# New hand-written orders for the four engines of a two-layer decoder kernel, with finer waits between its stages

## The reference, cut to what is computed

```python
x = x + L0_attn(layernorm(x))      # delta rule, 4 heads, RMS norm          } stage AB
x = x + L0_xattn(layernorm(x), ctx, ctx)   # causal, 16 heads of 8          }
x = x + L0_ffn(layernorm(x))       # depth 6: local attention, 16 heads of 64, rotary,
                                   # then a gated GELU layer                  stage C
x = x + L1_attn(layernorm(x))      # cosine attention, 16 heads of 8        }
x = x + L1_xattn(layernorm(x), ctx, ctx)   # mLSTM-like, 8 heads of 16      } stage DE
x = x + L1_ffn(layernorm(x))       # 16 experts, top 3, all experts computed}
```

## Time and profile before

| quantity | value |
|---|---|
| median of 3 runs | 4438.04 us (4435.57 to 4442.29) |
| the profiled execution, first to last instruction | 4433.1 us |
| PE busy, mean granted clock | 4137.5 us (93%), 0.969 |
| DVE, ACT, POOL busy | 3566.6, 3444.4, 2650.6 us |
| stage AB, from the start to its last addition | 0 to 546 us |
| stage C | 546 to 3485 us |
| stage DE | 3485 to 4433 us |

### The profile page before, as it was taken

The page is one execution under the profiler, slowest core; times in us unless marked ns, Lnnn a source line. Parts: engine busy times, 40 slices in busy tenths (PEclk is TensorE's granted clock), DMA queues, the critical chain, the costliest instruction groups (busy, mean ns, idle before and its releaser), DMA issues.

```text
span 4433.1 us, 150676 instructions
## 1 busy us (share of the span) xinstructions
PE 4137.5 (93%) x61520; PEld 3049.0 (69%) x61520; DVE 3566.6 (80%) x11101; ACT 3444.4 (78%) x9647; POOL 2650.6 (60%) x2210
## 2 busy tenths in 40 slices
PE   7999989999999999999999999999999689999999
PEld 5777756666666666666666666666666478888888
DVE  4666599999889888899898989898989357766775
ACT  3555478889888888888888988888888357776776
POOL 3444377777777777777777777777777133333331
PEclk8888899999999999999999999999999789999999
DMA  3000000000000000000000000000000100000000
GB/s 101 4 4 4 4 3 4 5 3 4 29 4 4 4 28 4 4 4 13 20 3 4 5 28 4 4 4 8 7 9 9 47 2 4 4 4 4 4 4 6
DMA packets 65258, 46.43 MB, mean 10 GB/s; under 512 B 29220, under 2 KB 63032, under 8 KB 63800
## 3 DMA queue, kind: packets, MB, share of 16 engines
q1 hardware_dynamic: 64568, 36.78, 2.9%
HBM read 28.48 MB, written 2.10 MB: 7 GB/s over the span
## 4 chain that ended last, share of the span: by engine, by line
PE 68%; ACT 13%; DVE 10%; POOL 5%; issue 5%; SPq 0%; DVEq 0%; DMA 0%; ACTq 0%; POOLq 0%
PE ps L557 56%; PE ps L561 12%; ACT BIG L909 7%; DVE BIG L1109 5%; POOL BIG L1549 5%; ACT L909 2%; ACT BIG L901 2%; DVE sm L1120 2%; ACT ps L901 1%; DVE BIG L1117 1%; DVE BIG L1114 1%; POOL sm L1552 0%; DVE sm L1117 0%; DVE BIG L1187 0%; DVE sm L1113 0%
## 5 line engine op out<-in xcount | busy, mean ns | idle before, releaser
L557 PE MATMUL ps<-WB,BIG 128*128 128x128 f32 (+2 forms) x8576 | 1941.9, 363 | 8.4 <-ACT BIG L901 3.4
L901 ACT ACTIVATE BIG<-ps 128x512 f32<-128x512 f32 (+6 forms) x3168 | 1484.0, 530 | 538.8 <-PE ps L561 407.7
L1549 POOL TENSOR_TENSOR BIG<-BIG,sm 128x512 f32<-128x512 f32 (+1 forms) x864 | 1219.0, 1426 | 788.7 <-DVE sm L1319 473.5
L557 PEld LDWEIGHTS ps<-WB,BIG 128*128 128x128 f32 (+1 forms) x8576 | 1142.2, 193 | 217.6 <-issue 175.6
L561 PEld LDWEIGHTS ps<-t_ident,BIG 128*128 128x128 f32 x6016 | 705.8, 144 | 541.4 <-issue 250.2
L561 PE MATMUL ps<-t_ident,BIG 128*128 128x128 f32 x6016 | 916.2, 282 | 162.5 <-ACT BIG L901 53.3
L1549 POOL TENSOR_TENSOR BIG<-BIG 128x512 f32<-128x512 f32 x768 | 967.2, 1280 | 144.1 <-DVE BIG L1109 144.1
L1120 DVE TENSOR_REDUCE sm<-BIG 128x8 f32<-128x512 f32 (+3 forms) x1472 | 882.6, 611 | 174.5 <-ACT BIG L909 172.2
L557 PEld LDWEIGHTS ps<-BIG 64*64 64x64 f32 (+2 forms) x37888 | 626.0, 130 | 364.6 <-issue 93.1
L557 PE MATMUL ps<-BIG 64*64 64x64 f32 (+4 forms) x37888 | 774.7, 225 | 69.7 <-ACT BIG L901 18.7
L909 ACT ACTIVATE BIG<-ps 128x512 f32<-128x512 f32 (+1 forms) x832 | 512.1, 616 | 257.3 <-PE ps L557 252.3
(11 more groups left out here) (120 smaller groups left out, 2985.1 us busy)
## 6 DMA issues: line engine op xcount, KB each, us to landing
WB<-in_Wqkv SPq DMA_DIRECT2D x6, 1536.0 KB, 7.4
XS<-y_sb SPq DMA_DIRECT2D x96, 63.0 KB
y_sb<-in_ctx SPq DMA_DIRECT2D x16, 256.0 KB, 3.1
WB<-in_Wo SPq DMA_DIRECT2D x6, 512.0 KB, 9.1
x_sb<-in_x SPq DMA_DIRECT2D x8, 256.0 KB, 5.0
WB<-in_F_W SPq DMA_DIRECT2D x1, 2048.0 KB, 8.6
WB<-in_F_W SPq DMA_DIRECT2D x8, 256.0 KB, 6.5
out<-x_sb SPq DMA_DIRECT2D x8, 256.0 KB, 2.3
```

The costliest lines, as they stand in the source:

```text
L557: return te.matmul(o, l, r, start=start, stop=stop, skip_group_check=not check)
L901: return se.activation(o, i, ACT.Copy)
L1549: return pe_.tensor_tensor(o, a, b, op)
```

## The change

All three order tables are new for all engines. The phases and their instructions stay the same, with these exceptions:

- C's first layer norm becomes phases of its own (`d1` to `d4` on DVE, `d` on POOL), run only for depth step 0; `first_norm`, `first_pow` and the two `rot` semaphores go.
- The table of rotary factors is made at DVE's first phase of tile 30 of the step before, not at slot start of tile 0.
- The barriers `all_ab` and `all_c` go. In their place a phase waits for the single phase that last used its buffer (`after_one`, `after_two` and the waits in `dve_de`). PE's banks are handed out through all stages in one pass.
- C's semaphores form a ring of 12 in place of 8, since its units now live for up to 9 slots.
- After the last GELU an ACT table set that holds both logarithm and exponential is loaded by hand.
- The expert weights are loaded in two parts, the first while C's last step runs.
- `SLOT` and `BEGIN` give every phase a number by which an engine's list is sorted. They lie so far apart that the stages stay in sequence on every engine.

The diff, cut to its core:

```diff
 AB_ORDER = {
-    "pe": "J1 b12 V3 s4 O3 a22 u5 b22 T1 o3 a32 w3 t5 G1 b32 D1 p14 a42 v4 x3 b42 X0 q3 Z2 y5 a11 W2 p04",
+    "pe": "V3 b12 s4 O3 u5 a22 o3 b22 T1 w3 a32 b32 G1 a42 D1 b42 v4 x3 X0 p14 t5 q3 Z2 a11 W2 y5 p04 J0",
...
 DE_ORDER = {
-    "pe": "om3 p12 oJ6 p02 av3 u2 hA5 oK6 t2 hO6 oL6 w2 hD5 hN6 oA5 gT5 hP6 oB5 b25 oC5 xc2 hG5 X11 hE5 oM6 g2 hF5 "
-          "oD5 J1 oP6 oN6 oO6 X34 oE5 hI5 hJ5 hH5 oF5 g34 cs2 oG5 hC4 hB4 T1 hK5 G2 s1 hM5 oI5 oH5 hL5 ct2",
-    "act": "h25 xc4 hG7 hE7 X13 kG7 kE7 hF7 g14 sq3 kF7 g24 X36 hI7 kI7 hJ7 hH7 kJ7 x36 kH7 T3 hC6 kC6 hB6 hK7 kB6 "
-           "kK7 e13 ex4 hM7 e03 kM7 hL7 ct4 kL7 p13 em4 p03 t3 hA6 hO7 vc1 kA6 kO7 hD6 hN7 gT6 kD6 hP7 kP7 kN7",
+    "pe": "oP7 hF6 xc3 hG6 oC6 oD6 hI6 oE6 g3 X35 oF6 oG6 hH6 g35 cs3 T2 hC5 hB5 hJ6 G3 s2 hK6 oI6 hM6 hA5 oH6 hL6 "
+          "p12 ct3 hD5 p02 hN6 av3 om3 oJ6 hP6 oL6 u2 oK6 X11 hO6 oM6 t2 gT5 oA5 w2 oN6 b25 J1 oO6 hE5 oB5",
+    "act": "g24 kI7 hH7 x36 kH7 hC6 T3 hJ7 hB6 kC6 kJ7 kB6 hK7 e13 ex4 e03 hM7 kM7 hA6 kA6 kK7 p13 hL7 ct4 hD6 kL7 "
+           "kD6 p03 hN7 kN7 em4 hP7 X12 kP7 t3 hO7 gT6 kO7 sq2 hE6 kE6 xc3 hF6 hG6 kF6 h24 vc3 kG6 X35 g13 hI6",
...
 C_ORDER = {
-    "pe": "2tr3 1v13 2a16 1k12 1p15 2o6 1o6 1b03 1a03 1q01 2g03 2g13 2g23 1b13 1a13 2a03 1v03 2a23 1p04 1q11 "
-          "1y5 1w5 1s3 1x0 1k01",
-    "act": "1b04 1q02 1a04 1b14 2g04 2g14 2g24 1f04 1f14 1a14 1q12 1v04 2sh2 1p05 1o06 1o16 1x1 1k02 1s04 1k12 "
-           "2tr3 1s14 1v13 1p15",
-    "dve": "1first0 1n42 1n52 1n62 1n72 1i14 1n82 2a23 1r01 1q11 1s03 1r11 2a15 1s13 1k01 1l01 1u03 1o5 1k11 "
-           "2sh1 2ag1 1i03 1l11 2o5 2ep1 1u13 1n01 1q00 1n11 1n21 2tr1 1n31 2a02 1second1",
-    "pool": "1first1 1n13 1q12 1k02 1q02 1p04 1k12 2sh2 1p14 1n02",
+    "pe": "1b06 1a06 2g26 2a26 1v06 1b16 2a18 2g16 1a16 1y8 1q14 1w8 1k04 1x3 1v15 2tr5 1s6 1p07 2g07 1k14 1o8 1p17 "
+          "2o8 2a07 1q03",
+    "act": "2sh5 1f07 1q05 1b07 1a07 1s18 1v07 1a17 1b17 1f17 2g27 1q15 2g17 1o09 1o19 1x4 1k05 2tr6 1v16 1p08 2g08 "
+           "1k15 1s07 1p18",
+    "dve": "1q04 1n05 1d10 1n15 1d20 1n25 1n35 1d30 1n45 1i07 1n55 1d41 2a18 2tr5 1u17 2a26 1n65 1n75 1i17 1n85 1r04 "
+           "1q14 1r14 1s06 1s16 2sh4 1k04 2ag4 2ep4 1k14 1o8 2o8 1l14 2a07 1l04 1u06",
+    "pool": "1q16 1n17 2sh6 1q06 1k06 1k16 1p08 1d1 1p18 1n06",
 }
...
+SLOT = {"ab": 14.8, "c": 11.6, "de": 25.4}
+BEGIN = {
+    "ab": {"pe": -0.7, "act": -3.5, "dve": -10.8, "pool": -18.7},
+    "c": {"pe": 1069.1, "act": 1060.6, "dve": 1071.2, "pool": 1059.6},
+    "de": {"pe": 4802.5, "act": 4787.2, "dve": 4783.2, "pool": 4816.1},
+}
...
-        CC = ring_units(kinds, "c", 8)
+        CC = ring_units(kinds, "c", 12)
...
-        def all_ab():
-
-            return [u.on("dve", "y") for u in AB[-8:]]
-
-        def all_c():
-            return all_ab() + [u.on("dve", "x") for u in uC2.values() if u.at["l"] == depth - 1]
-
+        def after_one(u):
+
+            return [AB[29 + 2 * u.at["t"]].on("pe", "w")] if AB and u.at["l"] == 0 and u.at["t"] < 2 else []
...
+        def schedule(e):
+
+            due = []
+            for seq, order, stage in ((AB, AB_ORDER, "ab"), (CC, C_ORDER, "c"), (DE, DE_ORDER, "de")):
+                items = [(o[:-1], int(o[-1])) for o in order[e].split()]
+                for n in range(len(seq) + 10):
+                    for j, (ph, lag) in enumerate(items):
+                        u = unit(seq, n - lag)
...
+                            due.append((BEGIN[stage][e] + SLOT[stage] * (n + j / len(items)), u, ph[1:] if stage == "c" else ph))
+            return [d[1:] for d in sorted(due, key=lambda d: d[0])]
...
+                    if u is last2 and ph == LAST_GELU:
+                        o.then_inc(u.name("act", ph, sems), 1)
+                        se.preload_act_table_set("natural_log_exp_and_others")
+                        return
...
-                        for s in all_c() if t == 0 else [DE[t - 8].on("dve", "xP")] if t >= 8 else []:
-                            w.wait_ge(*s)
+                        if t >= 8:
+                            w.wait_ge(*DE[t - 8].on("dve", "xP"))
+                        elif CC and t < 4:
+                            w.wait_ge(*uC1[(depth - 1, NT - 4 + t)].on("pe", "o"))
+                        elif CC and t == 4:
+                            w.wait_ge(*last2.on("dve", "tr"))
```

More of the change, by code:

```diff
@@ L107 @@
 C_ORDER = {
[7 rows of a table removed]
[7 rows of a table added]
 }
-SILENT = ("first", "second")
+NORM = ("d1", "d2", "d3", "d", "d4")
 for _kind in "12":
@@ L160, in __init__ @@
         self.base = dict(base)
-        self.marks = MARKS["C2f" if at.get("last") else kind]
+        self.marks = MARKS[kind + "f" if at.get("last") or at.get("l") == 0 and kind == "C1" else kind]
         self.count = dict.fromkeys(ENG, 0)
@@ L371, in de_bufs @@
             return b
-        def phases(order, seq, e, n):
-            for o in order[e].split():
-                u = unit(seq, n - int(o[-1]))
-                if u:
-                    yield u, o[:-1]
-        for seq, order, emptied, pairs in ((AB, AB_ORDER, AB_EMPTIED, AB_PAIRS), (DE, DE_ORDER, DE_EMPTIED, DE_PAIRS)):
-            full, turn = [()] * 8, 0
-            for u in seq:
-                u.bank, u.after = {}, {}
-            for n in range(len(seq) + 8 if seq else 0):
-                for u, ph in phases(order, seq, "pe", n):
-                    if ph not in emptied:
-                        u.after[ph] = ()
-                        continue
-                    wide = 1 + (ph in pairs)
-                    turn += turn % wide
-                    u.bank[ph], u.after[ph] = turn % 8, full[turn % 8] + (full[turn % 8 + 1] if wide == 2 else ())
-                    for i in range(wide):
-                        full[(turn + i) % 8] = tuple((u, *m.split()) for m in emptied[ph])
-                    turn += wide
@@ L408, in build, with take @@
+        full, turn, primed = [()] * 8, 0, [(), ()]
+        for u in AB + CC + DE:
             if u:
                 u.bank, u.after = {}, {}
[L410 to L426 removed]
+        def take(u, ph, marks, wide, banks):
+            nonlocal turn
+            turn += turn % wide
+            u.bank[ph], u.after[ph] = turn % banks, ()
+            for i in range(wide):
+                u.after[ph] += full[(turn + i) % banks]
+                full[(turn + i) % banks] = tuple((u, *m.split()) for m in marks)
+            turn += wide
@@ new lines, in build @@
+        order = schedule("pe")
+        places = [i for i, (u, ph) in enumerate(order) if u.stage == "c"]
+        for i, (u, ph) in enumerate(order):
+            banks = 6 if places and places[0] <= i <= places[-1] else 8
+            if places and i == places[0]:
+                primed = [full[6], full[7]]
+            u.after[ph] = ()
+            if u.stage == "ab":
+                if ph in AB_EMPTIED:
+                    take(u, ph, AB_EMPTIED[ph], 1 + (ph in AB_PAIRS), banks)
+            elif u.stage == "de":
+                if ph in DE_EMPTIED:
+                    take(u, ph, DE_EMPTIED[ph], 1 + (ph in DE_PAIRS), banks)
+            elif u.kind == "C1" and ph == "s":
+                u.bank.update({"s0": 6, "s1": 7})
+                full[6], full[7] = ((u, "act", "s0"),), ((u, "act", "s1"),)
+            elif u.kind == "C1" and ph == "y":
+                for h in "01":
+                    take(u, "y" + h, ("act o" + h,), 1, 6)
+                u.after["y"] = u.after["y0"] + u.after["y1"]
+            elif u.kind == "C2" or ph != "w":
+                take(u, ph, EMPTIED[u.kind[1] + ph], 1, 6)
@@ L690, in pe_bank @@
             def pe_bank(u, ph):
[L692 to L695 removed]
+                for v, e, m in u.after[ph]:
                     w.wait_ge(*v.on(e, m))
@@ L1562, in _ @@
             w.wait_ge("const", 2)
+            for r in (0, 64):
+                pe_.memset(XS[r:r + 1, :, 64:128], 0.0)
+            pe_.memset(c2_bufs().hT[64:96, 1024:1536], 1.0).then_inc(sems["ones"], 1)
+            w.wait_ge("ones", 1)
             def pool_ab(u, ph):
```

211 lines of the change are left out of this document (103 added, 108 removed), and 18 rows, old and new, of tables (AB_ORDER, DE_ORDER).

## The result

The changed kernel takes 4381.25 us (median of 4, 4376.92 to 4384.2), and the kernel before, run beside it, 4440.16 us (median of 4, 4435.57 to 4443.65). The ratio is 0.9868, 95% interval 0.9855 to 0.9881. The sign and the range were right, the size was not: 59 us came where I had forecast 147. The profiled execution is 4382.4 us long, at a mean granted clock of 0.963. Lines move with the diff: PE's matmuls L557 are now L564 and its transposes L561 are L568; DVE's L1109 and L1117 are L1126 and L1134; ACT's L901 and L909 are L907 and L915.

What follows compares the result with a forecast made beforehand. PE, busy 93% of the span, was taken as the bound, gains coming only from its idle time. 4433.1 - 55 (DE steady) - 20 (DE first slots) - 72 (C) = 4286.1, so median 4291 us, range 4195 to 4400.

Steps and rivals of the forecast that it cites:

- rival (3): C: ACT falls behind and PE waits before `k0` in each of 192 C1 units; 4536 us at 0.9 us each; chance 0.10.
- the mix: PE: alternating small and large matmuls was taken as free, adding nothing to PE's busy time.
- I count nothing for it: C: keeping DVE's all-SBUF work away from POOL was booked at 0, up to 55 us were DVE the bound.
- The wait goes: DE: PE's 1.20 us wait on DVE's `C` before `ct` vanishes, given 1.4 us more cover.
- My lower bound of 25 us: DE, steady part: the least gain, against 55 us forecast, if the `ct` or `hK` wait returns elsewhere.
- residual 0.35 before `p1`: DE: PE still waits 0.35 us a tile before `p1` for POOL's masked `m1`, bounds 0 and 0.6.
- the 0.15 at `cs`: DE: a new wait of 0.15 us a tile, as `cs3` follows `g3` after five phases, about 1.6 us.
- the first slots: DE's start: splitting one tile's chain over two lags shortens the first slots, gaining 20 us, bounds 0 and 35.
- under 20 us from `T` to `T`: DE's first tiles: a sign of the forecast, successive `T` starts under 20 us apart, against 26.5 us in the old list.
- three waits that I had named: AB: new PE waits before `b2`, `b3` and `a4`; without cover such a pair costs 0.2 to 0.5 us.
- The clock of 0.89 stays: AB: PE's granted clock stays at 0.89, the work around `u` being the same.
- From 4230 to 4345: Whole kernel: reach in us of the main forecast, 4291 us, with the bounds of its terms; chance 0.49.

Runs made afterwards that it cites:

- free banks: The changed kernel with each PE phase of DE taking the PSUM bank that comes free first, instead of the next in rotation: 4353.27 us, ratio 0.977.
- the swap: The changed kernel with DVE's `rg` in DE issued behind `C` instead of ahead of it: 4373.82 us, ratio 0.982.
- the profile in which it was short by itself: The changed kernel with eight PE phases of AB put back in the old sequence: 4435.55 us, ratio 0.9966.
- both experiments with small edits: The changed kernel with eight AB phases of PE in old sequence (4435.55 us), and, separately, with PE's `w` moved between `a3` and `b3` (4402.78 us).

## Why the prediction was wrong, point by point

The length of a phase "in its turn" is counted from the end of the phase ahead of it on PE to its own end, so that a wait is part of it.

- **C, the steady group.** Right: 58.8 us (forecast 58.7), no wait of 1.1 us, and rival (3), `k0` waiting for `v0`'s bank, did not occur. It came out right partly by luck, by two terms that I had wrong and that cancel: PE's idle time fell by more than forecast (82 us, not 72), and its busy time in a group rose from 57.8 to 58.2 us by the mix, which I took as free.
- **C, the borders of the steps.** The failed step: "I count nothing for it", of VectorE and GpSimd colliding. The diff moved six small products into POOL's busy stretch, and I put no price on where they went, though the earlier trace rows had the price of one, up to 1149 ns. It costs 22 us of C, nearly all at four of the five borders, shown by moving them away. Without it C would have come out at -71.
- **DE, `ct` and the bank.** The failed step: "The wait goes". It left `ct` (1.86 us in its turn before, 0.44 after), but a wait on `C` belongs to a bank as much as to an input. In the old list `ct` was also the eighth bank after `G`, so the two fell together and I saw only one. In the new list `G s` take four banks, `hK oI hM hA` the other four, and `oH` lands on `G`'s, which by the chain that I had worked out for `ct` myself is free only 3.9 us after `G`. PE waited 38.9 us for it; with free banks, and `rg` long only once, DE was 32 us shorter and the wait was gone, so the bank is shown. My lower bound of 25 us, "if one of the two waits comes back under another name", was the case that occurred, and its size was too kind.
- **DE, the table loads.** They went, and `hK` fell from 1.59 to 0.64 us in its turn. A tacit step here was that a microsecond of idle time removed is a microsecond of span. In the old order it failed: 30 us of idle time less gave 9 us. In the changed kernel the clock stayed at 0.99, and there it cost little beside the bank.
- **DE, `rg`.** Again the collision counted as nothing. It makes 14 to 18 of these 32 us, shown by the swap and by the profile in which it was short by itself.
- **DE, the rest of the tile.** With banks free it is 25.7 us, beside 25.3 forecast. The residual 0.35 before `p1` was right (0.41); the 0.15 at `cs` did not come; the 0.4 over are large phases that now stand behind small ones: `oJ`, `oK`, `hK` and `J` 0.19 us longer in their turns, `u` 0.10, `T` 0.15, less three others at 0.19 that no longer do.
- **DE, the first slots.** -14 for -20, and not without the order: under the old one the first tile takes 143.3 us. The sign that I gave, under 20 us from `T` to `T`, was wrong: 22.7, 25.4 and 25.9 us for 26.5, 27.8 and 29.4. Each slot gained 2 to 4 us, not 9.
- **AB.** Forecast 0 within -16 and +19, measured +24.5, outside. Of the three waits that I had named, the one before `b3` came in every tile (0.40 us), the one before `a4` in 8 of 22 and the one before `b2` not; the one before `o` (0.39) I had not named. They make the full-clock tile 0.7 us longer, a little beyond my upper bound of 0.6. The failed step is "The clock of 0.89 stays": it fell to 0.84, and the tiles that it made slow are some 14 of 22 us. That the order is the cause is shown; why this order lowers the clock is open, since both experiments with small edits moved waits and clock at once.
- **Borders of the stages.** 0, as forecast, for DE (the old order with the new borders takes 947 us for 945). At AB's end 7 us go with a clock of 0.57 for 0.81, whose cause is unexplained. It was not tried with barriers put back.
- **The reach.** "From 4230 to 4345" is not what the bounds of the terms add up to: that is 4201 to 4437 us, and the measured time lies within it.

In sum: of the 147 us forecast on the profiled execution AB took back 24.5, the tables 22, the bank with `rg` 32, the mix in DE some 12 and the first slots 6. That leaves 50.5, and the two profiled spans stand 50.7 apart.

## What to carry to other kernels

When a list of phases is reordered under banks that rotate, write down for each phase which phase held its bank before and when that one is read empty; a wait on a reader shows up wherever the rotation lands, and moving the phase that waits today moves only its name. A small all-SBUF operation on VectorE can cost as much as the GpSimd operation beside it (here 1.3 us for 0.2), so look at what stands right behind it. And do not book removed idle time of TensorE one to one: here 30 us of it, taken away alone, were worth 9, and 2 in the stage's own profile.
